# The order of three VectorE operations in each unit of a state-space scan loop

## The reference, cut to what matters

```python
dt = softplus(x_dbl[..., :DT_RANK] @ dt_proj_w.T + dt_proj_b)
A = -exp(A_log)
dA = exp(dt[..., None] * A)                       # decay of each channel and state
dBx = (dt * x)[..., None] * Bm[:, :, None, :]     # what enters each state
h = dA_t * h + dBx_t                              # over the tokens
y = einsum('bdn,bn->bd', h, C_t)                  # sum over the 16 states
return y + x * D
```

## Time and profile before

| | |
|---|---|
| median of the runs | 1400.57 us |
| the profiled execution, its time | 1403.03 us |
| its span | 1401.2 us |
| TensorE (PE) busy | 1299.3 us, 93% |
| GpSimd (POOL) busy | 970.6 us, 69% |
| VectorE (DVE) busy | 944.1 us, 67% |
| ScalarE (ACT) busy | 716.9 us, 51% |

### The profile page before, as it was taken

How to read it: one execution, slowest core, us unless ns; L and a number is a source line. 1 busy time by engine, 2 the same in 40 slices (tenths; PEclk the granted TensorE clock), 3 DMA queues, 4 the chain that set the end, 5 groups by cost and what they waited for, 6 DMA issues and landing times. The chain is left out here.

```text
span 1401.2 us, 16598 instructions
## 1 busy us (share of the span) xinstructions
PE 1299.3 (93%) x5300; PEld 779.0 (56%) x5300; DVE 944.1 (67%) x1154; ACT 716.9 (51%) x1263; POOL 970.6 (69%) x508
## 2 busy tenths in 40 slices
PE   8999989999998989899797878899999999999997
PEld 3443333344333333333343333357999999999996
DVE  3899999899999999989999999964111111111110
ACT  4888776678785667676767564411111111111111
POOL 1999999999999999999999999824222222222211
PEclk9999999999999999899999999999999999999999
DMA  5655555554555464555455554508888888888982
GB/s 197 189 165 168 168 165 167 164 165 159 182 171 183 145 186 152 164 165 177 158 180 187 182 176 140 192 4 332 304 319 306 318 316 324 307 317 318 318 313 47
DMA packets 105497, 290.33 MB, mean 207 GB/s; under 512 B 9649, under 2 KB 19506, under 8 KB 89922
## 3 DMA queue, kind: packets, MB, share of 16 engines
q1 hardware_dynamic: 95762, 271.17, 55.4%
q0 software_dynamic: 9648, 18.09, 6.4%
HBM read 271.41 MB, written 9.96 MB: 201 GB/s over the span
## 5 line engine op out<-in xcount | busy, mean ns | idle before, releaser
L434 PE MATMUL ps_y<-arena,ident 128*128 128x512 f32 x1024 | 501.2, 621 | 56.2 <-POOL arena L1180 55.8
L1180 POOL TENSOR_TENSOR arena<-arena 128x1024 f32<-128x1024 f32 x192 | 457.9, 2408 | 19.0 <-DVE arena L918 14.8
L434 PEld LDWEIGHTS ps_y<-arena,ident 128*128 128x128 f32 x1024 | 192.1, 196 | 325.8 <-issue 214.4
L1164 POOL TENSOR_TENSOR arena<-arena 128x1024 f32<-128x1024 f32 x127 | 304.2, 2396 | 6.9 <-issue 5.6
L717 ACT ACTIVATE ps_de<-arena,An 128x512 f32<-128x512 f32 x256 | 176.4, 689 | 225.7 <-DVE arena L915 224.9
L1231 POOL DMA_INDIRECT out_x<-arena x39 | 61.8, 1585 | 317.6 <-ACT arena L853 308.9
L899 DVE TENSOR_TENSOR ps_u<-ps_du,arena 128x512 f32<-128x512 f32 x256 | 178.7, 698 | 23.9 <-DVE arena L929 8.6
L1131 DVE TENSOR_TENSOR arena<-ps_du,arena 128x512 f32<-128x512 f32 x39 | 27.0, 692 | 232.1 <-PE ps_du L597 232.1
L717 ACT ACTIVATE arena<-arena,An 128x512 f32<-128x512 f32 x256 | 181.6, 709 | 0.0
L915 DVE TENSOR_TENSOR_SCAN arena<-ps_de,hlast,arena 128x512 f32<-128x512 f32 x128 | 163.1, 1274 | 1.0 <-ACT arena L717 1.0
L915 DVE TENSOR_TENSOR_SCAN arena<-ps_de,arena 128x512 f32<-128x512 f32 x128 | 155.3, 1213 | 3.8 <-ACT arena L717 3.8
(11 more groups left out here) (221 smaller groups left out, 1487.7 us busy)
## 6 DMA issues: line engine op xcount, KB each, us to landing
arena<-bc_scratch SPq DMA_DIRECT2D x256, 512.0 KB, 4.7
arena<-in_W SPq DMA_DIRECT2D x117, 1024.0 KB, 6.9
arena<-arena POOLq DMA_DIRECT2D x15, 512.0 KB, 5.0
arena<-in_xT SPq DMA_DIRECT2D x2, 1024.0 KB, 5.9
arena<-in_w2c SPq DMA_DIRECT2D x1, 2048.0 KB, 7.9
arena<-in_xT SPq DMA_DIRECT2D x4, 512.0 KB, 6.1
X_scratch<-stg SPq DMA_DIRECT2D x12, 128.0 KB, 4.8
out_x<-stg SPq DMA_DIRECT2D x12, 128.0 KB, 5.0
```

Of the source, the lines that this page charges most:

```text
L434: t = e.matmul(Y[j][:, :], ident[:, :], hc[:, i % NP, j, :], start=False, stop=(n == 15))
L1164: e.tensor_tensor(uA[:, turn % 2, :, :], duA.rearrange("p (o t) -> p o t", o=1).to_broadcast([128, 2, TH]), ring[:, turn % NR, 0, :, :], A ...
L1180: e.tensor_tensor(hc[:, i % NP, :, :], hh[:, i % NH, :, :], c, ALU.mult).then_inc(gp_hc, 1)
```

## The change: scan a comes first, then u, then scan b

The function that issued both scans is cut in two, and `u` is called between them. In unit 0 the weight product stays behind `u` and so comes between the scans, too. The instructions, their operands and the semaphores that they wait for are the same; `du` stays ahead of all three.

```diff
-            def scans(i):
+            def scan_a(i):
                 q, th, pr, n = unit(i)
                 e.wait_ge(ac_dA, i + 1)
...
                 e.tensor_tensor_scan(hh[:, i % NH, 1, :], DE[i % 2][:, :], uA[:, i // 2 % 2, i % 2, :],
                                      hlast[:, 2 * pr + 1, n:n + 1] if th else 0.0, ALU.mult, ALU.add).then_inc(dv_sA, 1)
+
+            def scan_b(i):
+                q, th, pr, n = unit(i)
                 e.wait_ge(dv_u, i + 1)
                 e.tensor_tensor_scan(U[:, :] if own(i) else hh[:, i % NH, 0, :], dA[:, i % ND, :], U[:, :],
                                      hlast[:, 2 * pr, n:n + 1] if th else 0.0, ALU.mult, ALU.add).then_inc(dv_sB, 1)
...
                 if i % 16 == 0:
                     du(i)
+                scan_a(i)
                 u(i)
                 if i == 0:
                     second_weights(0)
-                scans(i)
+                scan_b(i)
                 if own(i):
                     own_product(i)
                 small_work(i)
```

## The result

| | median | runs |
|---|---|---|
| before | 1400.59 us (1398.57 to 1402.83) | 10 |
| after | 1404.66 us (1403.13 to 1406.50) | 10 |

The ratio is 1.0031, 95% interval 1.0022 to 1.0041, so 4.1 us slower. A second comparison on another chip gave 1.0044 (1.0028 to 1.0060). The two traces are therefore only 0.6 us apart: they show which waits moved, and not the whole of the 4 us.

What follows compares the result with a forecast made beforehand. VectorE was taken to run nearly back to back in the loop, GpSimd hardly less. Of 11.4 us saved on VectorE 4.1 arrive; with +0.9 for the start and +1.0 for ScalarE, net -2.2 us: 1398, range 1390 to 1405.

Steps and rivals of the forecast that it cites:

- VectorE's units: VectorE's loop: u to scan b 0.72 us, own product to scan a 0.60, a plain unit 3.09 instead of 3.15.
- The sum of 11.4 us: VectorE's saving over 256 units: 8.6 from plain units, 7.2 behind own products, less 4.4 behind small work.
- Rival 2: Waits cost the same in either place, so VectorE gains nothing: +1.9 us, 1402.5; chance 0.10.
- rival 3: Scan b's wait on u is dear, 0.29 us each instead of 0.12: +32 us, 1433; chance 0.08.
- What of it arrives: Of VectorE's saving in the loop 4.1 us arrive: 0.8 in blocks 0 to 2, 3.3 in 3 to 6, 0 in 7.
- the first blocks: Blocks 0 to 2, of 32 units each: GpSimd sets the pace and only 0.8 us of 7.3 can arrive.
- a sign of it: Waits of scan a on GpSimd's u or product must appear in the first 100 us of the loop.
- The start: Units 0 and 1: scan b comes later, moving GpSimd's product of unit 1 from 47.74 to 48.6, +0.9 us.
- ScalarE: Later u holds ScalarE's copy into DU; this reaches scan a at one place, about +1 us, +12 if the cover fails everywhere.
- The hold at the copy: At each 16th unit ScalarE's copy into DU waits for u: held 1.1 us longer in 11 places, 5.4 to some 17 us.
- the cover: In the other ten copy places ScalarE waits for a scan again soon after, so the longer hold costs nothing.
- rival 4: TensorE's clock falls in other places, adding or taking one or two stops: -5 or +5 us; chance 0.20.

Runs made afterwards that it cites:

- the light kernels: The order of before, the changed kernel, and both, each without GpSimd's product of block 1 in every fourth unit: 1398.99, 1394.37 and 1387.88 us.
- both_light: Changed kernel with keep_last one unit later, u first in each 16th unit, and GpSimd's block 1 product left out in every fourth unit: 1387.88 us, ratio 0.9917.
- before_light: The kernel before, with GpSimd's product of block 1 left out in every fourth unit: 1398.99 us, ratio 0.9992.
- both: The changed kernel with keep_last issued one unit later and u first again in each 16th unit: 1402.68 us, ratio 1.0009.
- r_after: The changed kernel itself, measured once more against before on another chip: 1406.40 us, ratio 1.0044.
- before_holds: The kernel before with two ScalarE waits added: keep_last also waits for u, the copy into DU also for scan a: 1409.34 us, ratio 1.0056.
- both_ring: The kernel both, with the ring's rows of C not loaded again from the fourth turn on: 1396.37 us, ratio 0.9963.
- both_unit0: The kernel both, with unit 0 in its old order: 1397.85 us, ratio 0.9984; measured again on another chip, 1400.43 us, 0.9996.
- the first comparison: after_light against before_light: 1394.37 against 1398.99 us, 4.6 us faster by the medians.
- the second: both_light against before_light: 1387.88 against 1398.99 us, 11.1 us faster by the medians.
- after_ring: The changed kernel, with the ring's rows of C not loaded again from the fourth turn on: 1398.57 us, ratio 0.9989.
- before_ring: The kernel before, with the ring's rows of C not loaded again from the fourth turn on: 1401.03 us, ratio 1.0000.
- after_light: The changed kernel, with GpSimd's product of block 1 left out in every fourth unit: 1394.37 us, ratio 0.9950.

## Why the prediction was wrong

Forecast was 1398, 2.6 us faster; measured is 1404.7, 4.1 slower, still inside the range of 1390 to 1405. Point by point:

- *VectorE's units.* Right: u to scan b 0.71 for 0.72, own product to scan a 0.61 for 0.60. The sum of 11.4 us came to about 10, estimated from the traces: in the loops of the light kernels 7.8 us shorter beside 2.5 us more of waits for exponentials, and in after 0.9 shorter beside some 9 more of waits. That the medians of both_light and before_light differ by 11.1 is luck, since 4.7 us of it lie behind the loop. Rival 2 (waits cost the same) and rival 3 (a dear wait) are refuted by the same rows.
- *What of it arrives.* This was wrong in the reason given. GpSimd was to take up the saving from the first blocks on, and as a sign of it scan a was to wait for GpSimd's u or product in the first 100 us. In the trace of after that wait is 1.2 us, all in unit 0, and none from there to 150 us; VectorE waited for exponentials, 4.7 us between 40 and 150 us where it was 1.8. GpSimd does withhold something once the holds are mostly out, as both and both_light show. But after these edits 0.4 to 2.7 us arrived, where 4.1 was forecast, and the ring's loads, which the prediction left at a list of waits, account for some 6 us in the changed orders.
- *The start*, +0.9: about right in size (the wait 1.20 for "about 1.2", the product 0.65 later), with GpSimd's first u and not an exponential as what scan a waited for.
- *ScalarE*, "about +1". This is the step that failed, by its size and by a term that is missing. The hold at the copy was put at 1.1 us each. It is (24.4-5.4)/11 = 1.7, since ScalarE's exponentials start from scan a, which comes 0.6 earlier now, while u comes 1.1 later; "some 17 us" for the sum was 24.4. The wait of `keep_last` for scan b, another 29.1 us, I had not looked at: I followed the waits on the u that moved, but not those on scan b, which moved against scan a. And the cover, that ScalarE waits for a scan again soon after, rested on its being busy for half of the span. In the loop it is busy for 616 of 880 us, 70%, and wherever a table load or an activation stands in its queue the cover fails: VectorE waited for the exponentials in 18 places and not in 7, 10.9 us more in place of 1. Taken out, the holds give 3 to 4 us beside GpSimd and about 7 without it. The loop of before, with ScalarE's busy time in front of (x1073):
```profile
40.00:920.00 880.00, 798.14 (x1842) 331.42 (x1841) 837.83 (x948) 616.39 (x1073) 850.46 (x414) 0.97 0.53 167
```
- *TensorE's clock*, rival 4. It did not decide the change itself: VectorE's waits for TensorE's sums at the own product were 7.2 us after 7.8, and the mean granted clock was 0.975 to 0.981 in the ten runs of after (mean 0.978), and 0.9765 in r_after beside 0.9769 for before on its chip. But it did weigh in before_light, and may have in before_holds and both_ring.

The medians give +0.9 to +2.1 for the start and +3 to +5 for ScalarE, less the 0.4 to 2.7 that arrive: +1 to +7, around the 4.1 measured. This is no independent test, as it reads the same runs backwards. How the terms divide more finely stays open: the medians of one kernel moved by 2.6 us between chips (both_unit0).

## What to carry to other kernels

When an operation is moved within a unit, list every semaphore of the unit and ask for each waiter how far its release moved against the release that starts that waiter's work; the one that didn't itself move (scan b) can be the one that costs. An engine's busy share is to be taken from the part of the kernel that the edit touches (ScalarE: 51% of the span, 70% of the loop), and even then it may have no slack, where its queue has long pieces behind a short wait. Where two engines are busy for 95 and 97% of a loop, a run that leaves out a part of the other's work shows whether a gain can arrive. But the end of the loop has to be read in each trace as well, and not the median alone: here 4 us of the first comparison and 4.7 of the second came from another part of the kernel.

## What the runs showed of the hardware

- A VectorE multiply of 128x512 into PSUM with the scan that reads it waiting right behind it costs 0.71 us from start to start, against 0.60 where nothing waits; the price of that wait is 0.11 us, close to the 0.13 from du to u.
- The scan behind such a wait is itself 0.03 us longer (1.28 or 1.29 against 1.26), and u, with a scan in front of it, 0.02 to 0.03 shorter (0.67 or 0.68 against 0.70).
- With one 512 KB load to a ring slot instead of two, GpSimd's waits for the ring, 8.3 us in after (4.3 and 4.0), are gone from the view of after_ring. One such load took 4.7 us from issue to landing in before and 3.7 in before_ring (medians).
- With TensorE busy for 10.00 of 10 us, its granted clock was 0.71 from 930 to 940 us in before_light and 0.84 in after_light; the part behind the loop, the same in both, took 483.3 and 479.3 us.
